# Issuing the shift rows of three groups in four from ScalarE's DMA queue

## The chip, the cores and the metric

The kernel runs on one core of one Trainium2 chip. The metric is the device time of one execution in microseconds (us); the time of a kernel is the median of its runs.

## What is computed

One transformer block over 16 sequences (NB) of 512 tokens with 128 features, in fp32. The part that the change touches is the attention; behind it comes a mixture of eight experts with the two best chosen for each token.

```python
h = _layernorm(x) * (1 + ca) + sa
q, k, v = h @ Wq.T + bq, h @ Wk.T + bk, h @ Wv.T + bv      # 16 heads of 8
scores = einsum('bhqd,bhkd->bhqk', q, k) / sqrt(8)
out = einsum('bhqk,bhkd->bhqd', softmax(scores), v)
x = x + ga * (out @ Wo.T + bo)
h = _layernorm(x) * (1 + cb) + sb
x = x + gb * top2_of_8_experts(h)                          # silu(h @ wg) * (h @ wu) @ wd
```

## The kernel before, in words

**Tiles.** A batch `b` is one sequence. Its 16 heads go in four groups (`g` = 0 to 3) of four heads, and the work is cut into slots `k` = 0 to 15, four to a group; `hh` is the slot's place in its group and `t` one of four tiles of 128 tokens. A group has the running number `s = 4b + g`.

**Scores twice.** The softmax needs each row's maximum before the exponentials. TensorE therefore looks two groups ahead: for group `s + 2` it multiplies queries by keys (L826) and VectorE takes the row maxima (L1324, tile `maxes`). Later it computes the same scores transposed (L819, keys by queries), and ScalarE takes the exponentials of these (L1038). The maxima are subtracted inside that second product: fp32 queries and keys are stored as bf16 parts stacked in partitions (`q_st`, `k_st`), and two rows more of the stack hold the negated maxima, high and low part: the shift rows. `k_st` has ones in those rows.

**The way of a shift row.** VectorE makes `shift` from the maxima, TensorE transposes it (L760) at the end of slot `hh` = 0 of the group before, VectorE copies it out of PSUM to `shift_t` (L1170), and four DMAs of 2 KB each move it to its rows of `q_st` (L482, `stack_shift`), each adding 16 to `shift_stacked`. TensorE waits for 64 of these per group ahead of the group's first exponent product (L816).

**Banks.** Both products go through three PSUM banks in turn. The exponent product of tile `t` waits for the exponential of three tiles before. So TensorE can be at most three tiles ahead of ScalarE. In a slot TensorE's order is: for each tile L819, then L826; then eight products of probabilities by values (L839); then at most one step on the shared bank `misc`. Everything on an engine runs in this order, written out by hand.

**Miscellaneous steps.** Each batch also carries the projections of the batches ahead and the residual of the batch before. Those that matter: in slot 7 TensorE computes the output projection `y` (L771) and ScalarE drains it to `z` (L1023); this drain waits for `x_r` and `prm_t` of the batch before, both counted on `xr_loaded` (L1022). In slot 8, ahead of its first look-ahead product, TensorE waits until the next batch's stacks are all in (`stack_ready`, 18 DMAs, L823).

**SP's queue.** All plain DMAs go from SyncE's (SP's) queue in one written order. For batch `b` that order is:

```python
load_x_a(b + 2, d)        # L465, L466
stack_shift(b, 1, d)      # L482
store_parts(1, b + 1, d)  # L490: key parts to DRAM
load_stacks(b + 1, d)     # L514, L497, L500: 18 DMAs into q_st and k_st
load_x_r(b - 1, d)        # L472 (x_r), L473 (prm_t)
stack_shift(b, 2, d)
stack_shift(b, 3, d)
stack_shift(b + 1, 0, d)
store_x1(b - 1, d); load_row(b - 1, d)
store_parts(0, b + 2, d)
```

ScalarE and VectorE issue no DMA in this kernel; GpSimd issues the scattered rows of the expert part. Batches 4 to 13 run in a hardware loop of two batches a turn.

Of the kernel before, what the change touches and what calls it, by code (L numbers as in the profile page):

```python
# [38 lines left out]
NB, S, D = 16, 512, 128  # L39
NH, DK = 16, 8  # L40
NE, INTER = 8, 176
QT = S // P
# [8 lines left out]
NG = NH // GROUP  # L51
NS = NB * NG
TERMS = 6
SIDE = 64
SHIFT = TERMS * DK
# [39 lines left out]
def lin(f, n, d):  # L95

    if d is None:
        return f(n)
    assert f(n + 4) - f(n + 2) == f(n + 2) - f(n)
    return d * (f(n + 2) - f(n)) + f(n)  # L100


def wait(eng, sem, f, n, d):

    v = lin(f, n, d)
    if not isinstance(v, int) or v > 0:
        eng.wait_ge(sem, v)
# [6 lines left out]
def turn(i):  # L114

    last = NH * QT - 1
    before = i - TURN if i >= TURN else max(j for j in range(last + 1) if j % TURN == i % TURN) - last - 1
    return i % TURN, i - before
# [25 lines left out]
def misc_order():  # L144

    steps = [("hT", 0), ("q", 0), ("k", 0)]
    for b in range(-1, NB + 3):
        steps += [misc_at(b, k, end) for k in range(NH) for end in (0, 1) if misc_at(b, k, end)]
    return {step: i for i, step in enumerate(steps)}


def adaln_block(nc, x, Wq, bq, Wk, bk, Wv, bv, Wo, bo, gate_w, wg, wu, wd, c, wmod,
                ident_c, tri_c, rank_c, slots_c, map_c, place_c, out):
    with ExitStack() as ctx:
        def sb(name, shape, dt=F32):
            return ctx.enter_context(nc.sbuf_tensor(name, shape, dt))

        def sem(name):
            return ctx.enter_context(nc.semaphore(name))
# [53 lines left out]
        q_st = [[sb(f"q_st{i}_{side}", [P, PAIRS, S], BF16) for side in range(2)] for i in range(2)]  # L213
# [13 lines left out]
        shift = [sb(f"shift{i}", [P, 2, 2, 2, QT], BF16) for i in range(2)]  # L227
        shift_t = [sb(f"shift_t{i}", [4 * 2 * QT, P], BF16) for i in range(2)]
# [11 lines left out]
        row = [sb(f"row{i}", [P, ROW_G]) for i in range(2)]  # L240
# [13 lines left out]
        def parts(area):  # L254

            taken = [0]

            def part(n):
                taken[0] += n
                return area[:, taken[0] - n:taken[0]]  # L260
            return part

        part = parts(probs[:, :, :, :].rearrange("p a b s -> p (a b s)"))
# [13 lines left out]
        def stack(st):  # L277
            return st[:, :, :].rearrange("p j s -> p (j s)").bitcast(F32)

        x_in = [stack((q_st[0][0], k_st[0])[i % 2])[:, XW * (i // 2):XW * (i // 2 + 1)] for i in range(SLOTS)]  # L280
        part = parts(stack(q_st[0][1]))
# [38 lines left out]
        misc_drained = sem("misc_drained")  # L320
# [8 lines left out]
        shift_stacked = sem("shift_stacked")  # L329
# [41 lines left out]
        at = misc_order()  # L371
# [37 lines left out]
        def _(sp):  # L409
# [50 lines left out]
            def load_x_a(n, d):  # L460


                wait(sp, misc_drained, lambda n: at["hT", n - 1] + 1 if n > 1 else 0, n, d)
                b = batch_of(n, d)
                sp.dma_start(x_a[:, :, :], x[b].rearrange("(t p) d -> p t d", p=P)).then_inc(xa_loaded, 16)  # L465
                sp.dma_start(prm_a[:, :], prm_d[b]).then_inc(xa_loaded, 16)  # L466

            def load_x_r(n, d):

                wait(sp, misc_drained, lambda n: at["x1", n - 1] + 1 if n else 0, n, d)  # L470
                b = batch_of(n, d)
                sp.dma_start(x_r[:, :, :], x[b].rearrange("(t p) d -> p t d", p=P)).then_inc(xr_loaded, 16)  # L472
                sp.dma_start(prm_t[:, :], prm_d[b]).then_inc(xr_loaded, 16)  # L473

            def stack_shift(b, g, d):

                wait(sp, misc_drained, lambda b: at["shift", NG * b + g] + 1, b, d)
                for side in range(2):
                    for part in range(2):
                        row = SIDE * side + SHIFT + part  # L480
                        src = 2 * QT * (2 * side + part)
                        sp.dma_start(q_st[b % 2][side][row:row + 1, 2 * g:2 * g + 2, :],  # L482
                                     shift_t[g % 2][src:src + 2 * QT, :]).then_inc(shift_stacked, 16)

            def store_parts(i, n, d):

                b = batch_of(n, d)
                parts, dram = ((q_parts, q_parts_d), (k_parts, k_parts_d))[i]
                wait(sp, split_ready, lambda n: 2 * n + i + 1, n, d)
                sp.dma_start(dram[b].rearrange("t r s -> r t s"), parts[:, :, :]).then_inc(parts_stored[i], 16)  # L490
# [13 lines left out]
            def load_stacks(n, d):  # L504

                b = batch_of(n, d)

                if d is None and n <= 1:
                    sp.wait_ge(ones_stacked, 64)
                    sp.wait_ge(zeros_stacked, 128)  # L510
                both = [(side, SIDE * side, SIDE * (side + 1)) for side in range(2)]
                for side, lo, hi in both:

                    sp.dma_start(q_st[n % 2][side][lo + SHIFT:lo + SHIFT + 2, :, :],  # L514
                                 q_st[n % 2][1 - side][lo + SHIFT:lo + SHIFT + 2, :, :]).then_inc(stack_ready, 16)
                wait(sp, parts_stored[0], lambda n: 16 * (n + 1), n, d)
                for side, lo, hi in both:
                    for u, parts in enumerate(((0, 0), (1, 1), (0, 2))):
                        load_parts(q_st[n % 2][side], q_parts_d[b], lo, hi, u, parts)
                wait(sp, parts_stored[1], lambda n: 16 * (n + 1), n, d)  # L520
                for side, lo, hi in both:
                    for u, parts in enumerate(((1, 2), (1, 2), (0, 1))):
                        load_parts(k_st[n % 2], k_parts_d[b], lo, hi, u, parts)
# [27 lines left out]
            def batch(b, d=None):  # L551
                if b + 2 < NB and b >= 0:
                    load_x_a(b + 2, d)
                if 0 <= b < NB:
                    stack_shift(b, 1, d)
                if b + 1 < NB:
                    store_parts(1, b + 1, d)
                    load_stacks(b + 1, d)
                if b == -1:
                    load_x_a(1, d)  # L560
                if 0 <= b - 1 < NB:
                    load_x_r(b - 1, d)
                if 0 <= b < NB:
                    stack_shift(b, 2, d)
                if 0 <= b < NB:
                    stack_shift(b, 3, d)
                if b == NB - 1:
                    fill(0)
                if b + 1 < NB:
                    stack_shift(b + 1, 0, d)  # L570
                if 0 <= b - 1 < NB:
                    store_x1(b - 1, d)
                    load_row(b - 1, d)
                if b + 2 < NB:
                    store_parts(0, b + 2, d)
# [12 lines left out]
            for b in range(FIRST):  # L588
                batch(b)
# [369 lines left out]
        def _(act):  # L959
# [46 lines left out]
            def misc_drain(kind, n, d):  # L1006
# [16 lines left out]
                    ins = act.activation(z[:, :], misc, ACT.Identity, scale=prm_t[:, GA:GA + 1], bias=prm_t[:, GABO:GABO + 1])  # L1023
                ins.then_inc(misc_drained, 1)

            def slot(b, k, d=None):
                    g, hh = divmod(k, GROUP)
                    s = NG * b + g
                    for t in range(QT):
                        if hh == 0 and t == 1 and 0 <= s - 2 < NS:  # L1030

                            wait(act, pv_ready, lambda b: NG * b + g - 1, b, d)
                            if s - 4 >= 0:
                                wait(act, misc_filled, lambda b: at["o", NG * b + g - 4] + 1, b, d)
                            act.copy(o_aug[g % 2][:, :], ps[:, PV_BANK, :]).then_inc(pv_taken, 1)  # L1035
                        if 0 <= s < NS:
                            wait(act, st_ready, lambda b: QT * (NH * b + k) + t + 1, b, d)
                            act.activation(probs[:, g % 2, hh, S * t:S * (t + 1)], ps[:, ST_BANK + turn(QT * k + t)[0], :],  # L1038
                                           ACT.Exp, scale=SCALE).then_inc(exps_done, 1)
                        step = misc_at(b, k, 0)  # L1040
                        if t == 2 and step and step[0] == "h2T":
                            misc_drain(*step, d)
                    if k == 12 and 0 <= b - 2 < NB:

                        wait(act, route_step, lambda b: ROUTE_STEPS * (b - 2) + 13, b, d)
                        act.activation(odds[:, 0, :], top[:, 3, :], ACT.Exp).then_inc(odds_ready, 1)
                    if 7 <= k < 7 + QT and b + 2 < NB:
                        normalise(b + 2, d, [k - 7])
                    step = misc_at(b, k, 1)
                    if step and step[0] in ("hT", "q", "k", "v", "oT", "y"):  # L1050
                        misc_drain(*step, d)
# [575 lines left out]
```

## Time and profile before

| | before |
|---|---|
| median of 3 runs | 1501.66 us (1500.46 to 1507.6) |
| span of the profiled execution | 1502.3 us |
| busy TensorE, VectorE, ScalarE, GpSimd | 79%, 67%, 53%, 36% of the span |
| chain that ended last | TensorE 52%, DMA 14%, SP's queue 13%, VectorE 8%, issue 7% |
| TensorE waiting for `shift_t` to land in `q_st` | 162.7 us in 17 waits |

The profiled execution took 0.64 us more than the median of the runs. A busy share is an average over the attention (up to about 1220 us) and the experts (after it); a wait is read in the stage where it stands. "SPq" is SP's queue of DMA issues, "ACTq" would be ScalarE's.

### The profile page before, as it was taken

The numbers are of one execution on the slowest core, as the hardware profiler recorded it, in microseconds if no ns is written. First come the engines' busy times: TensorE is split into PE (matmuls) and PEld (weight loads), VectorE is DVE, ScalarE is ACT, GpSimd is POOL, SyncE is SP. The second block draws the span as 40 slices with busy tenths as digits, with TensorE's granted clock in tenths as the row PEclk, the third lists the DMA queues.
The fourth block names the chain that finished last, engine by engine and source line by source line (L and its number), as shares of the span: only waits on it lengthen the run. The fifth ranks groups of instructions, "written<-read, shape, count | busy, mean of one in ns | idle before, by whom it ended". The sixth has DMA issues, their size and how long they took to land.

```text
span 1502.3 us, 26903 instructions
## 1 busy us (share of the span) xinstructions
PE 1191.8 (79%) x6826; PEld 567.9 (38%) x6827; DVE 1003.2 (67%) x2668; ACT 802.5 (53%) x1740; POOL 542.6 (36%) x595
## 2 busy tenths in 40 slices
PE   4285887979597879787978797879797989899982
PEld 2022322323232323232323232323232348798981
DVE  7294776959485859585958595868686845445556
ACT  3054665646465556555655564656564666455541
POOL 7020212324132324141415050505050347788764
PEclk9597988989898989898989898989898999999996
DMA  8220202121212121111212121202020132335677
GB/s 222 68 54 22 73 20 77 30 76 51 83 30 76 35 71 44 61 50 55 55 49 59 46 65 39 72 34 82 22 80 22 30 83 80 91 105 150 173 212 196
DMA packets 132900, 110.55 MB, mean 74 GB/s; under 512 B 22549, under 2 KB 123010, under 8 KB 129538
## 3 DMA queue, kind: packets, MB, share of 16 engines
q1 hardware_dynamic: 124082, 91.37, 22.0%
q0 software_dynamic: 8704, 17.97, 3.6%
q8 instruction: 33, 0.54, 0.2%
q14 instruction: 81, 0.66, 0.1%
HBM read 66.07 MB, written 41.18 MB: 71 GB/s over the span
## 4 chain that ended last, share of the span: by engine, by line
PE 52%; DMA 14%; SPq 13%; DVE 8%; issue 7%; POOL 3%; ACT 2%; DVEq 0%; ACTq 0%; POOLq 0%
PE ps L839 13%; PE ps L819 11%; PE ps L826 11%; DMA q_st<-shift_t 11%; DVE maxes L1324 4%; SPq L482 4%; PE ps L891 3%; PE ps L908 3%; PE ps L765 2%; SPq L500 2%; PE ps L900 1%; DMA k_st<-k_parts_d 1%; POOL ys_d L1575 1%; SPq L473 1%; PE ps L751 1%
## 5 line engine op out<-in xcount | busy, mean ns | idle before, releaser
L1324 DVE TENSOR_REDUCE maxes<-ps 128x1 f32<-128x512 f32 x1024 | 665.0, 681 | 284.1 <-PE ps L826 269.6
L1038 ACT ACTIVATE probs<-ps 128x512 f32<-128x512 f32 x1024 | 548.0, 606 | 231.2 <-PE ps L819 217.8
L819 PE MATMUL ps<-q_st,k_st 128*128 128x512 bf16 x1024 | 406.9, 400 | 176.2 <-DMA q_st<-shift_t 162.7
L826 PE MATMUL ps<-k_st,q_st 128*128 128x512 bf16 x1024 | 411.4, 403 | 59.9 <-DMA k_st<-k_parts_d 29.7
L1506 POOL TENSOR_TENSOR q_parts<-q,one 128x512 bf16<-128x512 f32 x16 | 16.6, 1035 | 752.0 <-ACT q L1013 752.0
L839 PE MATMUL ps<-probs,v_aug 128*32 128x512 f32 x2048 | 285.3, 631 | 1.1 <-ACT o_aug L1035 1.1
L819 PEld LDWEIGHTS ps<-q_st,k_st 128*128 128x128 bf16 x1024 | 105.2, 103 | 360.4 <-DMA q_st<-shift_t 174.3
L826 PEld LDWEIGHTS ps<-k_st,q_st 128*128 128x128 bf16 x1024 | 103.2, 101 | 202.0 <-DVE maxes L1324 97.2
L1536 POOL DMA_INDIRECT xs_d<-h,rows_o x128 | 123.8, 967 | 36.9 <-issue 36.5
L1447 DVE COPY probs<-ps 88x256 f32<-88x256 f32 x144 | 60.4, 420 | 98.0 <-PE ps L900 92.1
L908 PE MATMUL ps<-wd_t,probs 88*128 x576 | 93.7, 286 | 0.0
L1023 ACT ACTIVATE z<-ps,prm_t 128x512 f32<-128x512 f32 x16 | 12.4, 777 | 147.8 <-DMA prm_t<-prm_d 146.0
L1575 POOL DMA_INDIRECT ys_d<-probs,k_st x72 | 70.5, 979 | 26.0 <-ACT probs L1089 12.6
L908 PEld LDWEIGHTS ps<-wd_t,probs 88*128 88x128 f32 x576 | 77.1, 194 | 4.6 <-issue 0.6
L839 PEld LDWEIGHTS ps<-probs,v_aug 128*32 128x32 f32 x2048 | 42.1, 111 | 95.6 <-issue 84.1
L1575 POOL DMA_INDIRECT ys_d<-probs,q_st x72 | 70.9, 984 | 19.0 <-POOL gone L1574 7.4
L891 PE MATMUL ps<-wg_t,probs 128*128 x288 | 73.0, 336 | 3.0 <-DVE probs L1451 2.0
L1079 ACT COPY probs<-ps 128x128 f32<-128x128 f32 x143 | 37.9, 265 | 63.8 <-PE ps L884 63.0
L891 PE MATMUL ps<-wu_t,probs 128*128 x288 | 67.8, 318 | 0.0
L900 PE MATMUL ps<-ident,probs 128*88 128x128 f32 x288 | 56.7, 279 | 11.2 <-DVE probs L1451 10.2
L1451 DVE TENSOR_TENSOR probs<-probs,ps 128x176 f32<-128x176 f32 x144 | 46.5, 323 | 9.6 <-ACT probs L1083 9.5
L891 PEld LDWEIGHTS ps<-wu_t,probs 128*128 128x128 f32 x288 | 49.9, 194 | 0.0
(203 smaller groups left out, 1356.9 us busy)
## 6 DMA issues: line engine op xcount, KB each, us to landing
k_st<-k_parts_d SPq DMA_DIRECT2D x96, 128.0 KB
q_st<-q_parts_d SPq DMA_DIRECT2D x128, 64.0 KB
q_parts_d<-q_parts SPq DMA_DIRECT2D x16, 384.0 KB, 2.9
k_parts_d<-k_parts SPq DMA_DIRECT2D x16, 384.0 KB
probs<-ys_d SPq DMA_DIRECT2D x24, 256.0 KB, 4.6
q_st<-xs_d SPq DMA_DIRECT2D x72, 65.0 KB
k_st<-xs_d SPq DMA_DIRECT2D x72, 65.0 KB
q_st<-q_parts_d SPq DMA_DIRECT2D x32, 128.0 KB
```

What stands on the lines that cost most here:

```text
L482: sp.dma_start(q_st[b % 2][side][row:row + 1, 2 * g:2 * g + 2, :], shift_t[g % 2][src:src + 2 * QT, :]).then_inc(shift_stacked, 16)
L819: pe.matmul(ps[:, ST_BANK + bank, :], k_st[b % 2][:, j, P * t:P * (t + 1)], q_st[b % 2][side][:, j, :], start=True, stop=True).then_inc(st ...
L826: pe.matmul(ps[:, S_BANK + bank, :], q_st[bs % 2][side_s][:, js, P * t:P * (t + 1)], k_st[bs % 2][:, js, :], start=True, stop=True).then_i ...
L839: mm = pe.matmul(ps[VW * i:VW * (i + 1), PV_BANK, :], v_aug[bp % 2][:, hh, GROUP * gp + i, :], probs[:, gp % 2, i, S * hh:S * (hh + 1)], s ...
L891: mm = pe.matmul(ps[:, GU_BANK + m % 2, INTER * i:INTER * (i + 1)], x_t[m % 2], w[:, :, :].rearrange("p c h -> p (c h)")[:, bass.ds(e * IN ...
L900: mm = pe.transpose(ps[0:HALF, HT_BANK, P * i:P * (i + 1)], hid[m % 2][:, HALF * i:HALF * (i + 1)], ident[:, :])
L908: mm = pe.matmul(ps[:, Y_BANK + m % 2, 0:D], hid_t[m % 2][:, P * i:P * (i + 1)], wd_t[:, bass.ds(e * 2 + i, 1), :].rearrange("p a d -> p ( ...
L1038: act.activation(probs[:, g % 2, hh, S * t:S * (t + 1)], ps[:, ST_BANK + turn(QT * k + t)[0], :], ACT.Exp, scale=SCALE).then_inc(exps_done, 1)
L1324: dve.tensor_reduce(maxes[g % 2][:, hs % 2, hs // 2, t:t + 1], ps[:, S_BANK + bank, :], AX.X, ALU.max).then_inc(maxes_done, 1)
L1447: dve.tensor_copy(hid_t[(m - 1) % 2], ps[0:HALF, HT_BANK, 0:2 * P]).then_inc(hidt_taken, 1)
L1536: pool.indirect_dma_start(xs_d, bass.IndirectOffsetOnAxis(ap=rows_o[:, v:v + 1], axis=0), h2[n % 2][:, v // QT, v % QT, :], None).then_inc ...
L1575: pool.indirect_dma_start(ys_d, bass.IndirectOffsetOnAxis(ap=x_in[m % SLOTS][:, D + 1:XW].bitcast(U32), axis=0), y_out[m % SLOTS], None).t ...
```

## The change

The stacking of group 1 of each batch stays on SP. That of groups 2 and 3 and of group 0 of the next batch leaves SP's order and is issued by ScalarE, at the start of slot `hh` = 1 of the group before, which is slots 5, 9 and 13 of a batch. ScalarE first waits on `misc_drained` until VectorE has copied that group's `shift_t`. The DMAs, their sizes and their semaphore are the same.

```diff
                 if 0 <= b - 1 < NB:
                     load_x_r(b - 1, d)
-                if 0 <= b < NB:
-                    stack_shift(b, 2, d)
-                if 0 <= b < NB:
-                    stack_shift(b, 3, d)
                 if b == NB - 1:
                     fill(0)
-                if b + 1 < NB:
-                    stack_shift(b + 1, 0, d)
                 if 0 <= b - 1 < NB:
                     store_x1(b - 1, d)
                     load_row(b - 1, d)
...
+            def stack_next_shift(b, g, d):
+
+                wait(act, misc_drained, lambda b: at["shift", NG * b + g + 1] + 1, b, d)
+                to, pairs = q_st[(b + (g + 1) // NG) % 2], slice(2 * ((g + 1) % NG), 2 * ((g + 1) % NG) + 2)
+                for side in range(2):
+                    for part in range(2):
+                        row = SIDE * side + SHIFT + part
+                        src = 2 * QT * (2 * side + part)
+                        act.dma_start(to[side][row:row + 1, pairs, :],
+                                      shift_t[(g + 1) % 2][src:src + 2 * QT, :]).then_inc(shift_stacked, 16)
+
             def slot(b, k, d=None):
                     g, hh = divmod(k, GROUP)
                     s = NG * b + g
+                    if hh == 1 and g and 0 <= s + 1 < NS:
+                        stack_next_shift(b, g, d)
                     for t in range(QT):
```

## Rows read from the trace of the kernel before

**Rows 1.** The page: the chain that ended last, share of the span by engine.
```profile
PE 52%; DMA 14%; SPq 13%; DVE 8%; issue 7%; POOL 3%; ACT 2%; DVEq 0%; ACTq 0%; POOLq 0%
```

**Rows 2.** Waits of the whole span: waiter, releaser, us in total, times, longest.
```profile
ACT z L1023 <- DMA prm_t<-prm_d: 146.0, 14, 15.7
PE ps L819 <- DMA q_st<-shift_t: 162.7, 17, 16.7
```

**Rows 3.** Chain of waits, 612 to 640 us: start, length, what.
```profile
618.34 10.06 DMA q_st<-shift_t
...
628.45 0.61 PE ps L819
```

**Rows 4.** SP's queue in time, 594 to 638 us: start, length, issue, count.
```profile
594.21 2.73 SPq L482 DMA_DIRECT2D q_st<-shift_t  x4
...
604.00 4.26 SPq L500 DMA_DIRECT2D k_st<-k_parts_d  x6
...
609.07 5.64 SPq L473 DMA_DIRECT2D prm_t<-prm_d  x1
614.82 22.17 SPq L482 DMA_DIRECT2D q_st<-shift_t  x8
```

**Rows 5.** Stages of 620 to 630 us: the last three columns are PEclk, DMA share, GB/s.
```profile
620.00:625.00 5.00, 0.00 (x0) 0.00 (x0) 0.00 (x0) 0.00 (x0) 0.00 (x0) 0.85 0.13 52
625.00:630.00 5.00, 1.55 (x4) 0.66 (x5) 0.48 (x1) 1.69 (x3) 0.00 (x0) 0.50 0.05 19
626.50:627.00 0.50, 0.00 (x0) 0.00 (x0) 0.00 (x0) 0.00 (x0) 0.00 (x0) 0.50 0.13 36
627.00:627.50 0.50, 0.00 (x0) 0.00 (x0) 0.00 (x0) 0.00 (x0) 0.00 (x0) 0.50 0.04 6
```

**Rows 6.** ScalarE in time, 575 to 680 us: start, length, instruction, [idle before, releaser].
```profile
607.31 2.06 ACT L1038 ACTIVATE probs<-ps 128x512 f32<-128x512 f32 x4 [0.21 <-PE ps L819]
...
627.70 0.78 ACT L1023 ACTIVATE z<-ps,prm_t 128x512 f32<-128x512 f32 x1 [10.17 <-DMA prm_t<-prm_d]
...
634.30 2.06 ACT L1038 ACTIVATE probs<-ps 128x512 f32<-128x512 f32 x4 [1.68 <-PE ps L819]
...
655.82 0.69 ACT L1013 ACTIVATE q<-ps,bias 128x512 f32<-128x512 f32 x1 [1.58 <-PE ps L751]
656.41 2.05 ACT L1038 ACTIVATE probs<-ps 128x512 f32<-128x512 f32 x4
```

**Rows 7.** TensorE in time, 575 to 680 us, same columns.
```profile
608.19 0.38 PE L819 MATMUL ps<-q_st,k_st 128*128 128x512 bf16 x1
...
617.28 1.13 PE L771 MATMUL ps<-o_t,w_t 128*128 128x512 f32 x2
628.45 0.61 PE L819 MATMUL ps<-q_st,k_st 128*128 128x512 bf16 x1 [10.04 <-DMA q_st<-shift_t]
...
631.97 1.93 PE L839 MATMUL ps<-probs,v_aug 128*32 128x512 f32 x8
633.68 0.26 PE L760 MATMUL ps<-identb,shift 128*32 128x128 bf16 x1
...
635.18 0.38 PE L819 MATMUL ps<-q_st,k_st 128*128 128x512 bf16 x1
...
649.75 0.38 PE L819 MATMUL ps<-q_st,k_st 128*128 128x512 bf16 x1
```

**Rows 8.** VectorE in time, 575 to 680 us: the copies of `shift_t`.
```profile
607.08 0.21 DVE L1170 COPY shift_t<-ps 32x128 bf16<-32x128 bf16 x1 [0.67 <-PE ps L760]
...
634.07 0.21 DVE L1170 COPY shift_t<-ps 32x128 bf16<-32x128 bf16 x1 [1.20 <-PE ps L760]
...
648.04 0.20 DVE L1170 COPY shift_t<-ps 32x128 bf16<-32x128 bf16 x1
```

**Rows 9.** Instructions on `q_st`: ns of one issue min/median/max, first and last start.
```profile
L482 SPq DMA_DIRECT2D q_st<-shift_t x256: 626/635/2453, 81.5 to 1201.7; - x128
L497 SPq DMA_DIRECT2D q_st<-q_parts_d x128: 274/295/480, 40.6 to 1114.2; - x128
```

## The prediction

> **What bounds the kernel now.** I read the page first: TensorE holds half of the chain that ended last, and DMA and SP's queue over a quarter [rows 1]. The waits of the whole span name the DMA: TensorE waits 162.7 us in 17 waits for shift rows to land [rows 2], about ten microseconds in each of the 16 batches. Then one batch, the one between 594 and 668 us, in the chain, by queue and by engine. The chain shows where the wait stands: 10.06 us of landing, then TensorE's first exponent product of slot 8 at 628.45 [rows 3]. In SP's queue the reader is to see why the rows are late: they stand behind the six loads of `k_st` and behind `prm_t`, whose issue alone held SP for 5.64 us, and leave only from 614.82 on [rows 4], though VectorE had them ready at 607.29 [rows 8].
>
> The same rows hold what speaks against the change. ScalarE waits in the same place, 10.17 us until 627.70, and for another transfer: `prm_t`, which its drain `z` needs [rows 6]; over the span that is 146.0 us in 14 waits [rows 2]. It was issued at 609.07, ahead of the moved rows [rows 4], so moving them frees it of nothing. And in the stages up to 627 us the DMA engines are busy at 0.13, two of sixteen, at a steady rate that ends near 627 us [rows 5]. These are stack loads still running, and TensorE needs the next batch's stacks for the product right behind the first of slot 8 (L823). Three transfers end within two microseconds: the stacks near 627, `prm_t` at 627.7, the shift rows at 628.4. Taking away the last uncovers the second.
>
> **The change, step by step.** *Removed from SP:* twelve issues a batch. SP's next work behind them (the store of `x1`, the row, the query parts) waits for later results in any case; I cost this at nothing. The cover is SP's own idle time; without it, it would be twelve times 0.63 us [rows 9], still off the path. The stack loads stand ahead of the moved rows and start when group 1's rows, which stay, have gone [rows 4]; they come no sooner.
>
> *Step 1, slot 8.* ScalarE still starts `z` at 627.70. Its next instruction can start 0.59 us later, as behind the drain of `q` (655.82 to 656.41) [rows 6], so the first exponential runs from 628.3 to 628.9. TensorE, with rows and stacks in place, has done its three tiles ahead by then at the half clock that the stage grants (0.50, so 1.2 GHz) [rows 5], and its fourth goes at 629.0. Eight products took 3.52 us there (628.45 to 631.97) [rows 7], 0.44 each, so the value products start near 629.9 in place of 631.97: **2.1 us gained**, and the next transposition L760 starts at 631.6 in place of 633.68.
>
> *Step 2, slot 9.* ScalarE now has four DMA issues ahead of its exponentials. No row shows an issue by ScalarE. The same four take SP 2.73 us [rows 4], 0.63 us each and gaps [rows 9]; the cheapest issue with `q_st` in it is 0.27 us [rows 9], the longest of the moved kind 2.45 us [rows 9]. I take 2.73 for the four, since it is the same instruction, and keep 1.1 (four times 0.27) below; above, a blocked queue is a rival of its own. Behind the waiting ScalarE stand the exponentials, and for these TensorE waits at its fourth tile. Before, VectorE's copy ended 0.60 us after L760's start (633.68 to 634.28) [rows 7, 8]. After: 631.6 and 0.6 is 632.2, issues until 634.95, first exponential until 635.55, fourth product at 635.6 in place of 635.18 [rows 7]: **0.4 us late**. The gain of step 1 is gone.
>
> *Step 3, slot 13.* VectorE's copy ends at 648.24 [rows 8], now 0.4 later. With 2.73 for the issues and 0.65 to the end of an exponential, the fourth product goes at 652.0 in place of 649.75 [rows 7]: **2.25 us late** in all. TensorE runs without a gap behind that point and has nothing to make it up with.
>
> *Step 4, slot 5.* The same block delays TensorE by 2.4 us (634.28 plus 2.73 plus 0.6 against 635.18, worked at slot 9), but it lies ahead of the wait that ends at 627.70. That wait covers it; without it, it would cost 2.4.
>
> Sum: batches 0 to 14 lose 2.25 us each, 34. Batch 15 loads no further stacks, has no such wait, and issues in slots 5 and 9 only: 2.4 each, 5. Together 39 on a span of 1502.3, which stands 0.6 above the median: **1540 us**. For a price p of one issue, steps 2 and 3 give 8p less 3.2 us a batch: even at 0.40 us. At 0.27, step 2 ends 1.2 us early, step 3 brings 0.2 back, and batch 15 pays 1.7: 15 times 1.0 less 1.7 is a gain of 13, 1488.
>
> The Trainium skill (DMA: Bandwidth & Descriptors, "Issuing engines are not separate DMA queues") says that issuing from a second engine only saves the first one's issuing time, and that all run on the same sixteen DMA engines. By that rule the change has 12 issues of SP's time to save and nothing on the wire; the waits above agree that the wire is what ends last.
>
> **The rivals.** *A, the forecast,* as above: 1540.
>
> *B, ScalarE's issues are held up in slot 5, or the rows don't escape the loads.* ScalarE would issue from 607.31 on [rows 6], just when SP is held: 5.64 us on `prm_t` [rows 4], up to 2.45 on a shift row [rows 9]. If something that both share is full, ScalarE's last row leaves near 617.5, where SP's did. TensorE's fourth product of slot 5 then goes at 618.1 in place of 608.19 [rows 7]. From there to the output projection it needs 9.1 us (617.28 less 608.19), and half of a half-clock slot more (5.2 us from 628.45 to 633.68, so 2.6) because it stood idle as long as before [rows 5, 7]. Slot 8 starts near 630.9, at full clock, and slot 9 at its old time: step 1 gives nothing, steps 2 and 3 cost 2.3 and 1.9, 4.2 a batch, 63 and 5: 1570. If the rows land only behind the loads, at 628.4, it is the same sum. For it: SP's blocked issue is in the trace. Against: it depends on how full the shared part is at 607, and ScalarE's issues may slip in before 609.
>
> The Trainium skill (Perfetto Trace Analysis, "DMA Instruction — HWDGE (DVE, Sync)") has the descriptor generator locked for one issuing sequencer at a time; that would be B's mechanism. No row here shows two sequencers issuing.
>
> *C, the other side: ScalarE issues cheaply.* It is one mechanism, the price p, in slots 9 and 13, and it decides at 0.40 us: below that, step 1's two microseconds outlast it. At 0.27 it gives 1488; lower still, TensorE's own pace bounds the gain at 1.2 a batch: 1484. For it: issues to the same tile that took 0.295 in the middle [rows 9]. Against: the very instruction that moves took 0.635, and never under 0.626.
>
> *D, no difference:* p near 0.4, or VectorE's slack taking up what steps 2 and 3 cost.
>
> *E, the wait is the rows' alone.* If `z` and the stacks were in by 618.4, TensorE would go on at once: 10.0 and 2.6 of half clock gained, three blocks of 2.4 lost, 5.4 a batch: 1421. Against it stand ScalarE's own wait [rows 6] and the DMA share up to 627 [rows 5]. That the change doesn't do what it says would look like D; the edit leaves no room for it.
>
> **How the numbers follow.** A 0.50, B 0.26, C 0.12, D 0.08, E 0.04. What measurement can tell from no change is about 0.5%, 7.5 us. Faster: C and E, 0.16. The same: D, 0.08. Slower: A and B, 0.76. The range reaches from the lower bound of the price, 1488, to somewhat over B, 1580; E and part of what lies beyond either end is left out.
>
> **What would show it.** In the changed profile: ScalarE's `z` still waits some eight to ten microseconds for `prm_t` (step 1), while TensorE's wait for `shift_t` is gone or names `k_st` or ScalarE. The rows of ScalarE's issues show p; with 0.6 or more, TensorE waits for ScalarE's exponentials by two microseconds in slots 9 and 13 (steps 2, 3). Under B the issues in slot 5 are longer than those in slot 9, and TensorE's long wait moves to slot 5. The forecast is wrong if ScalarE's issues are far under 0.4 us, or if `z` starts well before the old time.

## The result and the profile after

The changed kernel takes **1568.8 us** (median of 4 runs, 1563.66 to 1575.75) against 1503.24 us before, beside it on the same chip: 1.0444 times as long, 95% interval 1.0409 to 1.0480. The forecast was 1540 with a range of 1488 to 1580: the sign is right, and the loss of 66 us is 1.7 times the 38 that the steps gave.

The page and the waits of the whole span, after:

```profile
span 1573.8 us, 26903 instructions
...
PE 1233.0 (78%) x6826; PEld 574.5 (37%) x6827; DVE 1007.9 (64%) x2668; ACT 796.8 (51%) x1740; POOL 542.0 (34%) x595
...
PE 29%; DMA 22%; SPq 16%; DVE 11%; issue 10%; ACTq 5%; POOL 4%; ACT 2%; DVEq 1%; POOLq 0%
```

```profile
PE ps L820 <- DMA k_st<-k_parts_d: 117.3, 16, 30.2
PE ps L813 <- ACT probs L1045: 112.1, 57, 2.7
ACT z L1017 <- DMA prm_t<-prm_d: 101.9, 14, 13.2
```

and one row of the kernel before, of the same kind:

```profile
PE ps L826 <- DMA k_st<-k_parts_d: 29.7, 1, 29.7
```

The reader is to see three things. The long wait for shift rows [rows 2] is gone, and a wait for `k_st` has come in its place: same place, next transfer. Of its 117.3 us, 30.2 are one wait at the kernel's start, which the kernel before has too. The other 15 waits, one in each of batches 0 to 14, are 87.1 us, 5.8 each, where the shift rows held TensorE for about ten. ScalarE still waits for `prm_t`, 7.3 us a time where it was 10.4 [rows 2]. And TensorE's wait for ScalarE's exponentials, 112.1 us in 57 waits, most of them some two microseconds long (before: 11.9 us in 11), answers to the 47 blocks that ScalarE's issues put ahead of exponentials (three in each batch, none in the last batch's slot 13). "ACTq" now holds 5% of the chain.

One batch in time, from ScalarE (the columns are those of [rows 6]). It answers to the batch of [rows 6 to 8], and its `z` starts at 664.09 where that one's started at 627.70:

```profile
642.31 2.61 ACTq L1028 DMA_DIRECT2D q_st<-shift_t  x4
645.04 2.06 ACT L1045 ACTIVATE probs<-ps 128x512 f32<-128x512 f32 x4 [2.95 <-issue]
...
664.09 0.78 ACT L1017 ACTIVATE z<-ps,prm_t 128x512 f32<-128x512 f32 x1 [9.04 <-DMA prm_t<-prm_d]
...
668.82 2.64 ACTq L1028 DMA_DIRECT2D q_st<-shift_t  x4
671.58 2.06 ACT L1045 ACTIVATE probs<-ps 128x512 f32<-128x512 f32 x4 [3.90 <-issue]
...
686.91 2.61 ACTq L1028 DMA_DIRECT2D q_st<-shift_t  x4
```

The same batch from TensorE. Its first row is slot 8's first exponent product, which needs the moved shift rows; they were in more than seven microseconds before `k_st` was:

```profile
655.75 0.38 PE L813 MATMUL ps<-q_st,k_st 128*128 128x512 bf16 x1
663.34 0.60 PE L820 MATMUL ps<-k_st,q_st 128*128 128x512 bf16 x1 [7.21 <-DMA k_st<-k_parts_d]
...
666.43 1.94 PE L833 MATMUL ps<-probs,v_aug 128*32 128x512 f32 x8
...
672.23 0.39 PE L813 MATMUL ps<-q_st,k_st 128*128 128x512 bf16 x1 [2.03 <-ACT probs L1045]
...
672.94 1.94 PE L833 MATMUL ps<-probs,v_aug 128*32 128x512 f32 x8
...
678.65 0.66 PE L768 MATMUL ps<-ident,z 128*128 128x128 f32 x4
...
690.28 0.39 PE L813 MATMUL ps<-q_st,k_st 128*128 128x512 bf16 x1 [1.73 <-ACT probs L1045]
```

and VectorE's copies of `shift_t`:

```profile
668.58 0.21 DVE L1177 COPY shift_t<-ps 32x128 bf16<-32x128 bf16 x1 [1.25 <-PE ps L754]
686.67 0.20 DVE L1177 COPY shift_t<-ps 32x128 bf16<-32x128 bf16 x1
708.34 0.21 DVE L1177 COPY shift_t<-ps 32x128 bf16<-32x128 bf16 x1
```

Two rows of the kernel before that the comparison needs as well, TensorE's transposition of `z` in slot 10 and VectorE's copy in the next batch's slot 0:

```profile
640.01 0.66 PE L774 MATMUL ps<-ident,z 128*128 128x128 f32 x4
```

```profile
667.88 0.21 DVE L1170 COPY shift_t<-ps 32x128 bf16<-32x128 bf16 x1
```

In the table both kernels are counted from the start of `z`, in us:

| from `z` to | before | after | later by |
|---|---|---|---|
| slot 8's value products | 4.27 | 2.34 | -1.93 |
| slot 9's copy of `shift_t` done | 6.58 | 4.70 | -1.88 |
| slot 9's fourth exponent product | 7.48 | 8.14 | 0.66 |
| slot 10's transposition of `z` | 12.31 | 14.56 | 2.25 |
| slot 13's copy done | 20.54 | 22.78 | 2.24 |
| slot 13's fourth product | 22.05 | 26.19 | 4.14 |
| the next slot 0's copy starts | 40.18 | 44.25 | 4.07 |

Over fourteen batches the key parts' store comes every 76.4 us in place of 72.1, 4.3 a batch. `z` starts on average 31.1 us behind that store in place of 30.9: the loads ahead of it are as late as they were.

### The profile page after: what moved, and what is told of

It is laid out like the page before. It is cut to its first block, busy times and chain, and to the rows that moved or that the text cites. A ratio compares the mean times of both kernels' runs of the same rounds, so it can differ in the third digit from the quotient of the medians.

```text
span 1573.8 us, 26903 instructions
## 1 busy us (share of the span) xinstructions
PE 1233.0 (78%) x6826; PEld 574.5 (37%) x6827; DVE 1007.9 (64%) x2668; ACT 796.8 (51%) x1740; POOL 542.0 (34%) x595
## 2 busy tenths in 40 slices
DMA packets 132900, 110.55 MB, mean 70 GB/s; under 512 B 22549, under 2 KB 123010, under 8 KB 129538
## 4 chain that ended last, share of the span: by engine, by line
PE 29%; DMA 22%; SPq 16%; DVE 11%; issue 10%; ACTq 5%; POOL 4%; ACT 2%; DVEq 1%; POOLq 0%
DMA k_st<-k_parts_d 20%; PE ps L833 7%; ACTq L1028 5%; DVE maxes L1331 5%; PE ps L813 5%; PE ps L820 5%; SPq L500 5%; PE ps L885 3%; SPq L497 3%; PE ps L902 2%; SPq L482 2%; PE ps L759 2%; POOL ys_d L1582 2%; ACT probs L1045 1%; PE ps L894 1%
## 5 line engine op out<-in xcount | busy, mean ns | idle before, releaser
L820 PE MATMUL ps<-k_st,q_st 128*128 128x512 bf16 x1024 | 415.6, 407 | 147.3 <-DMA k_st<-k_parts_d 117.3
L813 PE MATMUL ps<-q_st,k_st 128*128 128x512 bf16 x1024 | 410.8, 404 | 117.8 <-ACT probs L1045 112.1
L833 PE MATMUL ps<-probs,v_aug 128*32 128x512 f32 x2048 | 303.2, 667 | 1.1 <-ACT o_aug L1042 1.1
L1182 DVE RECIPROCAL o_rs<-ps 128x16 f32<-128x16 f32 x64 | 16.5, 258 | 81.5 <-PE ps L759 81.5
L894 PE MATMUL ps<-ident,probs 128*88 128x128 f32 x288 | 56.9, 280 | 11.3 <-DVE probs L1458 10.4
L759 PEld LDWEIGHTS ps<-ident,o_aug 128*128 128x128 f32 x256 | 32.7, 164 | 72.2 <-issue 71.8
```

What stands on the lines that cost most here:

```text
L813: pe.matmul(ps[:, ST_BANK + bank, :], k_st[b % 2][:, j, P * t:P * (t + 1)], q_st[b % 2][side][:, j, :], start=True, stop=True).then_inc(st ...
L820: pe.matmul(ps[:, S_BANK + bank, :], q_st[bs % 2][side_s][:, js, P * t:P * (t + 1)], k_st[bs % 2][:, js, :], start=True, stop=True).then_i ...
L833: mm = pe.matmul(ps[VW * i:VW * (i + 1), PV_BANK, :], v_aug[bp % 2][:, hh, GROUP * gp + i, :], probs[:, gp % 2, i, S * hh:S * (hh + 1)], s ...
L894: mm = pe.transpose(ps[0:HALF, HT_BANK, P * i:P * (i + 1)], hid[m % 2][:, HALF * i:HALF * (i + 1)], ident[:, :])
```

## The experiments

The experiments ran on three chips, and the chips differ. The kernel before took 1576.44 us beside the first four runs (group 2 alone, groups 3 and 0, two issues a group, issues in idle time), 1507.86 beside the next four (the changed kernel again, the two with spread stacks, the residual's loads moved) and 1574.23 beside the last four (group 3 alone, group 0 alone, the two combinations). So only ratios to the kernel before on the same chip are compared, and ratios of different chips with care; what the slower chips do is told at the end.

**Which of the three blocks costs.** First came group 2 alone from ScalarE, then groups 3 and 0 alone:

```diff
-                    if hh == 1 and g and 0 <= s + 1 < NS:
+                    if hh == 1 and g == 1 and 0 <= s + 1 < NS:    # group2_only
+                    if hh == 1 and g > 1 and 0 <= s + 1 < NS:     # groups_3_and_0_only
```

with the other groups' `stack_shift` back in SP's order.

> Only group 2's rows (slot 5) go from ScalarE; groups 3 and 0 of the next batch are back on SP. Theory (ScalarE's blocked time costs in slots 9 and 13, slot 5 is covered by the wait for the stacks and prm_t): step 1's gain is kept, 0 to 2.1 us a batch, so 1470 to 1503 us, and z still starts about 31 us after the key parts' store. Rival (sharing two queues slows the loads or the issues in slot 5): over 1520, with z later than 32 us behind that store. Rival (the clock loses wherever ScalarE blocks TensorE for some two microseconds, slot 5 too): 1505 to 1520.

Measured: ratio 1.0002 (0.9964 to 1.0040).

> Group 2's rows are back on SP; groups 3 and 0 go from ScalarE in slots 9 and 13. Theory: nothing is gained in slot 8, and both blocks cost in full, 2.4 and 1.9 us a batch, plus what the clock adds: 1503 + 15 x 4.3 = 1567 without a clock loss, up to 1590 with 1.3 us a batch for it. Rival (slot 5 is what costs in the changed kernel): under 1530.

Measured: ratio 1.0567 (1.0503 to 1.0631), 89 us, at the end of the expectation that has a clock loss in it. So the issues in slot 5 are as good as free, and the whole loss lies in slots 9 and 13. The gain of step 1 is another matter. Measured as 1.9 us in each of 15 batches (the table above) it would be 1.8% of that kernel, and group 2 alone shows at most 0.4%. The change with all three groups loses less, 1.0444 on another chip, than groups 3 and 0 without group 2. The second rival of group 2 alone, a clock loss behind slot 5's block, is not excluded. What takes step 1's gain on this chip stays open. In the run with groups 3 and 0, TensorE's weight loads wait for shift rows again, half as long as in the profile of the kernel before (174.3 us there, on a faster chip):

```profile
PEld ps L815 <- DMA q_st<-shift_t: 85.0, 16, 16.5
```

Later the two were taken apart (`g == 2` and `g == 3` in the same line).

> Only group 3's rows (slot 9) go from ScalarE, the others from SP. The changed kernel lost 4.3 us a batch where steps 1 to 3 summed to 2.25; this prices step 2 without step 1's gain. Theory (the block alone): 2.5 us a batch, 16 batches, ratio 1.024 to 1.030. Rival (the block also costs clock in that slot, some 1.3 us): ratio 1.036 to 1.045.

Measured: ratio 1.0289 (1.0252 to 1.0325), 45.5 us, 2.8 for each of 16 batches.

> Only group 0 of the next batch (slot 13) goes from ScalarE. Theory (the block alone): 1.9 us a batch, 15 batches, ratio 1.016 to 1.022. Rival (the block also costs clock, or delays VectorE's work of that stage): ratio over 1.028.

Measured: ratio 1.0269 (1.0239 to 1.0298), 42.3 us, 2.8 for each of 15. The sum, 88, is that of the run with both, so the blocks add. Slot 9 came out as its theory said, near the upper end; slot 13 lies between its theory and the rival, 0.9 us above the block. The interval reaches over the rival's bound of 1.028, so this run leaves the rival standing and does not say what the 0.9 is.

**What makes a block dear.** Two issues a group in place of four:

```diff
-                    for part in range(2):
-                        row = SIDE * side + SHIFT + part
-                        src = 2 * QT * (2 * side + part)
-                        act.dma_start(to[side][row:row + 1, pairs, :],
-                                      shift_t[(g + 1) % 2][src:src + 2 * QT, :]).then_inc(shift_stacked, 16)
+                    row = SIDE * side + SHIFT
+                    src = 4 * QT * side
+                    act.dma_start(to[side][row:row + 2, pairs, :],
+                                  shift_t[(g + 1) % 2][src:src + 4 * QT, :]).then_inc(shift_stacked, 32)
```

> The changed kernel, but ScalarE moves a group with two DMAs of two rows in place of four of one. Theory (price is per issue, 0.63 us): each block is 1.3 us shorter; two blocks a batch on the path, 15 batches: 1569 - 40 = about 1529, and down to 1510 if the clock stays up too. Rival (price is per byte or per row): an issue takes 1.2 us and the time stays at 1560 to 1575.

Measured: ratio 1.0057 (1.0029 to 1.0086). That is more than the shorter blocks give (1568.8 less 40 us would be 1.017 times the kernel before), and near the end of the expectation where the clock stays up too. The price is per issue and not per row: the instructions on `q_st` show ScalarE's issue of one row in the changed kernel and of two rows here, ns minimum, median and maximum:

```profile
L1028 ACTq DMA_DIRECT2D q_st<-shift_t x192: 627/627/1232, 82.0 to 1269.0; - x192
```

```profile
L1027 ACTq DMA_DIRECT2D q_st<-shift_t x96: 620/621/1249, 81.9 to 1220.8; - x96
```

Twice the bytes and rows cost no more. (The 192 issues are 48 blocks of four: the first stands ahead of batch 0, with no exponentials behind it.) Then the same twelve issues where ScalarE is idle anyway:

```diff
-                    if hh == 1 and g and 0 <= s + 1 < NS:
-                        stack_next_shift(b, g, d)
...
                     if step and step[0] in ("hT", "q", "k", "v", "oT", "y"):
                         misc_drain(*step, d)
+                    if hh in (1, 2) and g and 0 <= s + 1 < NS:
+                        stack_next_shift(b, g, hh - 1, d)    # one side, two issues
```

> The changed kernel with the same 12 issues a batch, but two behind the exponentials of the group's second slot and two behind those of its third, where ScalarE stands idle 0.5 to 1.7 us a slot. Theory (the cost is the place ahead of four exponentials, not the issues as such): most of the cost goes, 1480 to 1520. Rival (twelve issues more on ScalarE cost their time wherever they stand): over 1550.

Measured: ratio 0.9857 (0.9788 to 0.9926), a little faster than the kernel before. All twelve issues are still ScalarE's, so it is not the issues as such that cost. The edit does two things at once, though: it moves the issues behind the exponentials and cuts the block of four into two of two. The run before had one block of two ahead of the exponentials and took 1.0057; here twice as many issues stand behind them and it takes 0.9857. So the place alone is worth at least 2%, and the length of the block the rest. TensorE's wait for ScalarE's exponentials has fallen from 112.1 us:

```profile
PE ps L813 <- ACT probs L1043: 41.1, 46, 2.4
```

**What ends last in slot 8.** The changed kernel once more, on the faster of the three chips:

> The changed kernel once more, beside the others on one chip. All theories: 1.044 times the kernel before, with the attention ending about 70 us later than before.

Measured: ratio 1.0420 (1.0393 to 1.0448). The attention's last product starts at 1278.9 us against 1219.4 in the profile before, 60 later where about 70 was expected. Beside it the stack loads spread wider, in the kernel before and in the changed one:

```diff
-                    sp.dma_start(st[lo + 2 * DK * u:lo + 2 * DK * (u + 1), :, :].rearrange("p j s -> p (j s)"),
-                                 dram[first:second + 1:second - first, lo:hi, :].rearrange("t (e j) s -> t e (j s)", e=DK)
-                                 ).then_inc(stack_ready, 16)
+                    for t, part in enumerate(parts):
+                        sp.dma_start(st[lo + DK * (2 * u + t):lo + DK * (2 * u + t + 1), :, :],
+                                     dram[part, lo:hi, :].rearrange("(e j) s -> e j s", e=DK)).then_inc(stack_ready, 16)
```

> The kernel before, but each stack load of 16 partitions from two parts is cut into two of 8 partitions from one part (26 DMAs a batch, not 18), so that they run on more of the DMA engines than the two that the trace shows busy at the end. Theory (all three transfers that end near slot 8 wait for those two engines): the waits for shift rows and for prm_t go, 10.0 + 2.6 us a batch, 15 batches, ratio 0.87 to 0.91. Rival (SP's issuing order alone makes the rows late): the wait stays at 8 us or more and the ratio is over 0.98.

Measured: ratio 0.8943 (0.8887 to 0.8998), 159 us less. Stages of the kernel before with spread stacks, the same columns as [rows 5] (length; busy time of TensorE, its weight loads, VectorE, ScalarE and GpSimd; granted clock, DMA share, GB/s):

```profile
535.00:540.00 5.00, 5.00 (x38) 2.46 (x36) 4.02 (x9) 3.40 (x8) 3.84 (x4) 1.00 0.59 142
540.00:545.00 5.00, 4.89 (x34) 1.83 (x27) 3.67 (x9) 3.55 (x8) 2.89 (x4) 1.00 0.67 173
545.00:550.00 5.00, 5.00 (x33) 2.49 (x31) 3.62 (x8) 3.27 (x8) 0.00 (x0) 1.00 0.47 137
550.00:555.00 5.00, 4.86 (x28) 1.50 (x27) 4.24 (x15) 4.01 (x9) 0.00 (x0) 1.00 0.00 0
```

The share is 0.47 to 0.67 and then nothing, where [rows 5] show 0.13 for many microseconds; TensorE is busy through all four stages, at full clock. Its waits for shift rows and ScalarE's for `prm_t`:

```profile
PE ps L819 <- DMA q_st<-shift_t: 33.4, 8, 12.2
...
ACT z L1023 <- DMA prm_t<-prm_d: 18.6, 4, 6.1
```

The bytes moved are the same, 110.55 MB before and 110.56 here. So the tail on two engines held all three transfers; SP's order alone leaves 33 of 163 us.

> The changed kernel with the same cut of the stack loads. Theory: the cover of slot 5 is gone too, so ScalarE's three blocks cost in full: 2.4 + 2.4 + 1.9 and up to 2 us of clock a batch, 100 to 130 us more than the kernel before with spread stacks, ratio 0.94 to 0.98. Rival (the second queue is what frees the rows, and with free transfers its cost is hidden): within 20 us of the kernel before with spread stacks.

Measured: ratio 0.9713 (0.9686 to 0.9739), 0.077 more than with the issues on SP. That is 116 us, 7.3 for each of 16 batches. With the cover gone the third block is paid too, as forecast: 2.4, 2.4 and 1.9 are 6.7. The two profiles say the same block by block. On average over batches 0 to 12, the way from the copy of `shift_t` to the fourth exponent product is 2.7 us longer in slot 9, 2.0 in slot 13 and 2.5 in slot 5. In the changed kernel with the old stack loads slot 5 is 2.5 longer as well, but the way from there to `z` is 2.1 shorter. That is step 4 shown.

> The kernel before, but SP loads x_r and prm_t ahead of the key parts' store and the stacks. Theory: ScalarE's wait for prm_t (146 us) goes and the time stays, ratio 0.99 to 1.01, since TensorE still waits for rows and stacks behind the same loads. Rival (z's parameters are the bound): 10 us and more faster.

The edit moves `load_x_r(b - 1, d)` ahead of `store_parts(1, b + 1, d)` in SP's order. Measured: ratio 0.9986 (0.9970 to 1.0001), and ScalarE no longer waits for `prm_t` (its `z` follows TensorE's product), while TensorE's wait for shift rows stays:

```profile
ACT z L1023 <- PE ps L771: 15.7, 16, 1.3
...
PE ps L819 <- DMA q_st<-shift_t: 159.7, 17, 16.7
```

Taking away one of three waits that end together gives nothing here. The change took away another one and gained 1.9 us in slot 8, the distance to the next.

**Both together.** Spread stacks with ScalarE's issues in its idle time, for all three groups and for group 2 alone (`g == 1` in the idle-time line, the others on SP).

> Spread stack loads, and all three groups from ScalarE in its idle time (two issues behind the second slot, two behind the third). Theory: the 33 us that the kernel before with spread stacks still waits for shift rows go, ScalarE's issues give back 10 to 30: ratio 0.875 to 0.900. Rival (ScalarE has no room left once the wait is gone): over 0.91.

Measured: ratio 0.9556 (0.9517 to 0.9596).

> Spread stack loads, and only group 2 from ScalarE in its idle time; groups 3 and 0 stay on SP. Theory: the remaining waits for shift rows go and little is given back: ratio 0.865 to 0.890, the best of all. Rival (as before): over 0.895, so no gain over spreading alone.

Measured: ratio 0.9535 (0.9495 to 0.9576). Both miss their theories and lie where the rivals put them, over 0.91 and over 0.895. But they ran on a chip where the kernel before takes 1574.23 us, and the spread alone did not run there, so the rivals are not shown either. Whether either beats the spread alone is open; both beat the kernel before.

## Why the prediction was right, and where it was short

*What bounds the kernel.* Right. The three transfers that end within two microseconds are shown by the two runs that free one of them (group 2 alone, and the residual's loads moved ahead) and gain nothing, and by the one that spreads the stack loads over more engines and removes most of all three. One count was off: the ten microseconds stand in 15 batches, not 16; the two other waits of the 17 are 1.6 and 1.0 us long.

*Step 1* said 2.1 gained; 1.93 measured. *Step 2* said 0.4 late in slot 9; 0.66. The four issues took 2.64 where 2.73 was taken from SP's row, 0.627 each. So the bound of 0.27 below came from the wrong neighbour: for this kind of issue ScalarE pays what SP pays.

*Step 3* priced slot 13's block at 1.85 on top of what came with it; from copy to fourth product it took 3.41 (686.87 to 690.28) in place of 1.51 [rows 7, 8], 1.9 more. Right as well on this chip; on the slower one slot 13 alone cost 2.8.

*The term that was missing* is the clock behind a block. In the batch shown it lies between slots 9 and 10: 6.42 us from the fourth product to the transposition of `z` (672.23 to 678.65), where the kernel before took 4.83 (635.18 to 640.01), 1.6 more. The stages say why (columns as above):

```profile
669.00:672.00 3.00, 1.20 (x5) 0.29 (x3) 2.18 (x6) 0.42 (x1) 0.00 (x0) 0.98 0.01 2
672.00:676.00 4.00, 3.77 (x15) 1.38 (x16) 0.83 (x3) 2.02 (x5) 0.00 (x0) 0.57 0.00 1
676.00:680.00 4.00, 4.00 (x24) 1.62 (x23) 3.40 (x8) 2.88 (x6) 0.00 (x0) 1.00 0.00 0
```

TensorE had stood still behind ScalarE, and the granted clock fell again, 0.98 to 0.57 (1.2 GHz most of the time, of 2.4), on work this time: eight value products took 1.94 us in place of 1.07. In the long wait before, much of the half clock lay on an idle engine. The prediction costed a block at its own length and left out what the clock takes after it. Over the span TensorE's busy time grows from 1191.8 to 1233.0 us with the same 6826 instructions. In this batch the account is -1.93 (step 1), 2.59 (slot 9's block with its surroundings), 1.59 (clock), 1.9 (slot 13), and -0.1 for the rest: 4.1, against the 2.25 forecast.

Not every batch loses it there. In the changed profile this stretch takes 6.4 to 6.5 us in six of batches 0 to 13 and 4.84 in the other eight, where the clock stays at 1.00. In some batches the clock falls behind slot 13's block, and the way to the next slot 0's copy of `shift_t` takes 17.4 us in place of 16.1. Three stages of the changed kernel: slots 9 and 10 of the next batch, then the way behind slot 13 with the fall and without it:

```profile
749.00:755.00 6.00, 5.82 (x37) 2.39 (x38) 3.81 (x10) 4.47 (x11) 0.00 (x0) 1.00 0.00 0
...
611.60:629.00 17.40, 15.58 (x72) 4.61 (x72) 14.09 (x36) 10.29 (x20) 8.82 (x8) 0.92 0.14 38
765.70:781.80 16.10, 14.28 (x72) 4.54 (x72) 14.11 (x36) 10.29 (x20) 8.83 (x8) 1.00 0.15 42
```

On average over batches 0 to 12 the stretch behind slot 9 is 0.75 us longer than before and the one behind slot 13 is 0.60 longer; the two blocks are 2.5 and 2.0, slot 8 gives back 2.0, and 0.3 lies elsewhere: 4.1 a batch. So about 1.3 of the 1.9 that the forecast was short of lie in the two stretches behind the blocks, where the clock falls. No run holds the clock fixed, and why it falls in one batch and not in the next stays open.

*Rival B* (1570) met the number and not the mechanism. ScalarE's four issues of slot 5 took 2.61 us, as long as those of slot 13, and nothing of TensorE's wait moved to slot 5 beyond the block's own 2.35 us. They were out at 644.92, while SP's issue of `prm_t` was held from 644.17 for 6.32 us. That overlap is short; in an earlier batch all four went out while SP was held, at 0.65 us each:

```profile
644.17 6.32 SPq L473 DMA_DIRECT2D prm_t<-prm_d  x1
...
254.74 5.94 SPq L473 DMA_DIRECT2D prm_t<-prm_d  x1
254.74 2.60 ACTq L1028 DMA_DIRECT2D q_st<-shift_t  x4
```

The rule of one locked descriptor generator (the Trainium skill, Perfetto Trace Analysis, "DMA Instruction — HWDGE (DVE, Sync)") may hold for each issue, but SP's held issue did not hold ScalarE's here. The moved rows were also in well before the loads ended: the product that needs them started at 655.75, and TensorE's wait, until 663.34, names `k_st`. That B's number is nearer than the forecast's is chance.

*Rival C* needed a price under 0.40 us; it is 0.63. *Rival E* fails by the wait for `k_st`. *Step 4* stands. The cost of nothing for SP's later work was not tested by itself.

## What to carry to other kernels

Before taking away a wait, look for what else lands at the same place, on every engine: a second engine waiting there, or a DMA share that stays at one or two engines' worth, says that the wait will change its name and stay. Price a DMA issue on a compute engine by the same issue on SP: here both took 0.63 us, for one row or for two. Ahead of work that another engine waits for it was paid in full, and more where TensorE's clock fell behind the stop; in ScalarE's idle time it was nearly free. Look at how few engines a load runs on: cutting eight loads differently brought 159 us, where step 1 of the change could have brought 15 times 1.9, 29 us.

## What the runs showed of the hardware that was not expected

**Few engines.** The eight stack loads of two parts each became sixteen of one part (26 DMAs a batch in place of 18), and the DMA share went from 0.13 to between 0.47 and 0.67. That agrees with the Trainium skill (DMA: Bandwidth & Descriptors, "Why a DMA increments its semaphore by 16 and not by 1"): a transfer is split over the largest number of engines up to 16 that divides both sides' slowest dimension, so the old loads, whose outer source dimension is 2, would run on two, and 0.13 of sixteen is two.

**An issue runs beside an exponential.** With the issues behind the exponentials, ScalarE's queue issues while the last of them is still running:

```profile
541.79 0.69 ACTq L1028 DMA_DIRECT2D q_st<-shift_t  x1
541.86 0.62 ACT L1043 ACTIVATE probs<-ps 128x512 f32<-128x512 f32 x1
```

**Two kinds of chip.** On two of the three chips of the experiments the kernel before is 4 to 5% slower. Two things are seen in the profiles from them. From the start of the attention's last exponent product to the end it takes some 350 us (1503.4 less 1152.9 with spread stacks and group 2) in place of 283. And in some batches TensorE, VectorE and ScalarE stop for nine to eleven microseconds around slot 4, while the stacks are loading. GpSimd and SP do not stop: in the batch shown GpSimd issues its eight scattered rows from 625.51 to 635.36. ScalarE in the run with group 3 alone:

```profile
638.31 0.58 ACT L1014 COPY v_aug<-ps 128x512 f32<-128x512 f32 x1 [10.84 <-remote]
```

Such a stop lies under the same cover as slot 5's block, so there is less of a wait to win there. That fits the smaller gain of the last two runs and the missing gain of group 2 alone, but no run tests it, and what stops the engines was not found.
